# A finished attention tile is scaled on GpSimd instead of VectorE, with double-buffered sums and a signal of its own for the banks

## The chip, the cores and the metric

The kernel runs on one core of a Trainium2 chip. The time is device microseconds (us) of one execution; a kernel's time is the median of its runs. A core has TensorE (PE, matmuls and transposes through its matrix array, into banks of PSUM), VectorE (DVE), ScalarE (ACT), GpSimd (POOL) and SyncE (SP, which here only issues DMAs). Each engine runs its own instructions in order; they order one another by semaphores.

## The reference, cut to what matters

A small language tower: a token embedding; four encoder layers with 12-head attention over a band of 64 keys on either side and a gelu feed-forward; a channel attention; a mixture of four experts; then one layer of full attention with 12 heads of 16 over 256 keys; then a mixture of eight experts. The batch is 8 sequences of 256 tokens, width 192, all float32. The change touches the last step of both attentions:

```
probs = jax.nn.softmax(scores, axis=-1)
out = einsum('bhcqk,bhckd->bhcqd', probs, vb)
```

The kernel doesn't divide the probabilities: it multiplies the exponentials with the values, gets each head's row sum beside them (the values carry a column of ones), and scales the 16 outputs of each head by the reciprocal of the sum afterwards.

## The kernel before, in words

The 2048 tokens are 16 tiles of 128 queries (`NT`); a sequence is two tiles. Attention goes over pairs of heads: 6 pairs to a tile, 96 pairs to a layer, `p` = 0 to 95, in four pair groups of 24 (a group is two sequences, four tiles). It runs five times: banded in the layers called 0 to 3 here, and once dense, with 256 keys. The same code writes the order for every engine:

- TensorE (`pe_attention`), in iteration `p`: scores of pair p (L534, L537), values of pair p-5 (L566 to L568), transposes of the probabilities of pair p-3 (L548), then in some iterations a step (`pe_step`) of work for the next pair group: three "chunks" of queries and keys (k = p mod 24 = 0, 2, 8), four tile transposes (k = 4, 6, 10, 12), four value projections (k = 14, 16, 18, 20). In the last pair group there are none of these; the banded layers have transposes of finished tiles and output projections there instead (`LATE`).
- ScalarE (`act_attention`): the exponentials (L660), and the high parts of the transposed probabilities, `pth` (L670).
- VectorE (`dve_attention`), in iteration p: the row maxima of pair p (`dve_max`, L766), the remainders `ptl` of pair p-4 (`dve_lo`, L772), its share of TensorE's last step, in pairs 6 to 13 of a banded layer the last normalisation of the layer before (`dve_last_norm`, L822 to L831), and then `dve_finish`. That one takes tile t in three parts: at p = 11 + 6t the sums to `rs2` (L786 or L790) and the values to `au` (L791), at p = 12 + 6t the reciprocals (L794), at p = 13 + 6t the scaling to `xn` (L799, 192 columns; L800 repeats the last 64 of them). L800 signals `att_ready`.
- GpSimd: it splits the next group's chunks into three bf16 pieces (`pool_pieces`, L1018 to L1021), which SyncE sends to DRAM and reads back as `qx` and `kx`; it splits the values (`pool_v`, L1084 to L1087), adds residual rows to `hb` (L967), and splits weights for the next stage (`pool_weights`, L999 to L1003: those of `wb` in pair group 1, those of `wa` at the start of pair group 3). Each of them waits, in order, for what it reads.

`att_ready` is waited for by TensorE ahead of the first values of a tile (the bank was used two tiles before), by ScalarE ahead of a tile's first exponential (the maxima of three tiles before), and by TensorE ahead of the transpose of the scaled tile, which comes in the last pair group or after the pairs.

Of the kernel before, what the change touches and what calls it, by code (L numbers as in the profile page):

```python
# [24 lines left out]
ALU = mybir.AluOpType  # L25
# [93 lines left out]
def build_tower(nc, a, out, stop=None):  # L119
    ctx = ExitStack()  # L120
    with ctx:
# [30 lines left out]
        rs2 = sb("rs2", [P, 2, HEADS])  # L152
        au = sb("au", [P, HEADS, DH])
# [14 lines left out]
        tok = au[:, 0, :].bitcast(I32)  # L168
        tokf = qf[:, 0, 0:2 * NT].rearrange("p (a n) -> p a n", a=2)
        toku = au[:, 1, :].bitcast(U32)  # L170
# [117 lines left out]
        att_ready = sig("att_ready", per=NT)  # L288
# [263 lines left out]
        def pe_values(pe, it, p):  # L552
# [4 lines left out]
            if p % 6 == 0:  # L557
                pe.wait_ge(att_ready.sem, att_ready.at(it, 2 * b + qt - 1))
# [90 lines left out]
        def act_exp(act, it, u, banded):  # L649
# [6 lines left out]
            if hd == 0:  # L656
                act.wait_ge(att_ready.sem, att_ready.at(it, tile_no - 2))
# [119 lines left out]
        def dve_finish(dve, ch, it, t, step, banded):  # L777

            r3, r = t % 3, rs2[:, 1, :]
# [56 lines left out]
        def dve_attention(dve, ch, it, banded, tile):  # L836

            for p in range(PAIRS + 8):
# [7 lines left out]
                if p >= 11 and (p - 11) % 6 < 3 and (p - 11) // 6 < NT:  # L846
                    dve_finish(dve, ch, it, (p - 11) // 6, (p - 11) % 6, banded)
# [122 lines left out]
        def pool_tail(pool, ch, it, opening):  # L970
# [9 lines left out]
            scale(1, 0)  # L980
# [24 lines left out]

        def pool_pieces(pool, ch, it, g):

            for i in range(3):
# [13 lines left out]
                pool.wait_ge(next_pieces.sem, next_pieces.at(it, n - 2))  # L1022

# [49 lines left out]
        def pool_v(pool, ch, it, g):  # L1073

            for i in range(4):
# [12 lines left out]
                pool.wait_ge(v3_ready.sem, v3_ready.at(it, n + 1))  # L1088

# [577 lines left out]
        def _(pool):  # L1667
            ch = Chain(ctx, nc, pool, "pool_order", alone)
            for s in (v3_ready, xc_pow_ready, seg_q_ready):
# [25 lines left out]
            def pool_layer(it, opening):  # L1695
# [9 lines left out]
                pool_v(pool, ch, it, 3)  # L1705
# [452 lines left out]
```

## Time and profile before

| | |
|---|---|
| time, median of 3 runs | 1967.51 us (1963.2 to 1977.52) |
| the profiled execution | 1966.12 us, of which the span of the trace is 1964.3 us |
| granted TensorE clock, mean | 0.898 |
| busy over the span | PE 1532.7 us, DVE 1340.6, ACT 1026.9, POOL 712.5 |
| the five stretches of pairs, first to last maximum | 80.4 to 238.5, 351.5 to 508.2, 621.2 to 777.7, 887.3 to 1040.9, 1480.4 to 1628.9 us |

The time of an execution is the trace's span and 1.8 us around it. Busy shares are means over stages with different limits; the rows below are read by stretch. In a timeline row the columns are start, duration, engine, line, operation, what it writes and reads, and in brackets the idle time of the engine just before it with what ended it. Durations of successive instructions of an engine overlap a little, so what an instruction costs is read from start to start.

### The profile page before, as it was taken

The page shows a single profiled execution, that of the slowest core. Times are in us where ns is not written, and L with a number is a line of the kernel's source. Part 1 is how long each engine was busy: PE and PEld are TensorE (multiplying, and loading weights), DVE is VectorE, ACT ScalarE, POOL GpSimd, SP SyncE. Part 2 cuts the span into 40 slices and gives each one's busy share as a digit, 9 for nine tenths or more (in the row PEclk, how much of TensorE's full clock was granted, in tenths as well). Part 3 has the DMA queues.
Part 4 walks back from the last instruction along what each step waited for, and adds up shares of the span by engine and source line. Part 5 has one row for each costly group of instructions (what it writes and reads, how often), then busy time and mean ns, then how long its engine had stood idle before and what let it go on. Part 6 is the DMA issues. An engine that isn't in the chain of part 4 may idle for free.

```text
span 1964.3 us, 45857 instructions
## 1 busy us (share of the span) xinstructions
PE 1532.7 (78%) x14634; PEld 1290.7 (66%) x14634; DVE 1340.6 (68%) x3638; ACT 1026.9 (52%) x2392; POOL 712.5 (36%) x993
## 2 busy tenths in 40 slices
PE   0689889789798898898897938849818886669992
PEld 0467668677677776786776827729816664569992
DVE  4698966789876989668997662253358998344444
ACT  0478733688534787337884313225417883235661
POOL 5554123553134641236531320024525421045541
PEclk9899989899898999899998968769958997679996
DMA  5645101634004451016430000046526430067775
GB/s 130 185 108 115 28 1 31 163 76 87 1 2 128 85 116 28 1 32 160 88 74 1 1 13 1 1 142 189 168 72 140 85 63 23 22 200 241 239 219 173
DMA packets 144329, 178.46 MB, mean 91 GB/s; under 512 B 22096, under 2 KB 106128, under 8 KB 143952
## 3 DMA queue, kind: packets, MB, share of 16 engines
q1 hardware_dynamic: 136784, 158.18, 31.6%
q0 software_dynamic: 7296, 17.18, 2.6%
q8 instruction: 129, 2.11, 0.5%
q14 instruction: 120, 0.98, 0.2%
HBM read 132.96 MB, written 42.34 MB: 89 GB/s over the span
## 4 chain that ended last, share of the span: by engine, by line
PE 31%; DVE 14%; issue 4%; ACT 2%; DMA 2%; POOL 1%; SPq 0%; DVEq 0%; ACTq 0%; POOLq 0%
PE bank L1414 7%; DVE ptl L772 4%; DVE neg_max L766 2%; PE bank L1400 2%; PE bank L548 2%; PE bank L618 2%; DVE xn L886 1%; PE bank L1403 1%; DMA xn<-y_rows 1%; PE bank L1401 1%; PE bank L1402 1%; PE bank L1404 1%; PE bank L423 1%; PE bank L1158 1%; ACT pth L670 1%
## 5 line engine op out<-in xcount | busy, mean ns | idle before, releaser
L660 ACT ACTIVATE prob<-bank,neg_max 128x192 f32<-128x192 f32 (+1 forms) x960 | 408.1, 436 | 132.2 <-DVE neg_max L766 79.0
L772 DVE TENSOR_TENSOR ptl<-bank,pth 128x512 f16<-128x512 f32 x480 | 327.0, 681 | 11.8 <-ACT pth L670 5.6
L766 DVE TENSOR_REDUCE neg_max<-bank 128x2 f32<-128x384 f32 (+1 forms) x480 | 273.4, 570 | 77.5 <-PE bank L537 68.7
L548 PE MATMUL bank<-ident,prob 128*128 128x128 f32 x1920 | 309.6, 285 | 0.0
L670 ACT ACTIVATE pth<-bank 128x512 f16<-128x512 f32 x480 | 284.8, 593 | 7.8 <-PE bank L548 7.5
L566 PE MATMUL bank<-v,pth 128*128 128x33 bf16 x1920 | 200.8, 181 | 106.7 <-DVE ptl L772 89.6
L566 PEld LDWEIGHTS bank<-v,pth 128*128 128x128 f16 x1920 | 154.7, 96 | 190.5 <-DVE ptl L772 177.5
L625 ACT ACTIVATE xx<-bank 128x256 fp32r<-128x256 f32 x256 | 95.7, 387 | 239.8 <-PE bank L423 235.6
L548 PEld LDWEIGHTS bank<-ident,prob 128*128 128x128 f32 x1920 | 205.1, 142 | 0.1
L568 PE MATMUL bank<-v,ptl 128*128 128x33 bf16 x1920 | 194.9, 177 | 0.0
L567 PE MATMUL bank<-v,pth 128*128 128x16 bf16 x1920 | 191.0, 170 | 1.9 <-issue 1.9
L960 POOL TENSOR_SCALAR rstd<-mv 128x4 f32<-128x4 f32 x52 | 12.9, 248 | 446.3 <-DVE mv L876 440.3
L537 PE MATMUL bank<-kx,qx 96*128 96x192 bf16 (+1 forms) x960 | 168.0, 257 | 1.1 <-DVE xx L739 1.1
L567 PEld LDWEIGHTS bank<-v,pth 128*128 128x128 f16 x1920 | 157.6, 97 | 0.1
L568 PEld LDWEIGHTS bank<-v,ptl 128*128 128x128 f16 x1920 | 155.4, 96 | 2.1 <-issue 2.1
L706 ACT ACTIVATE fbuf<-bank,b 128x512 f32<-128x512 f32 x96 | 65.9, 687 | 146.5 <-PE bank L445 146.5
L618 PE MATMUL bank<-w,fbuf 128*128 128x192 f32 x768 | 140.8, 327 | 2.0 <-DVE h L863 2.0
L423 PE MATMUL bank<-ident,xn 128*128 128x128 f32 x256 | 57.3, 339 | 104.6 <-DVE xn L886 54.0
L534 PE MATMUL bank<-mask,ident 128*128 128x384 bf16 x384 | 130.2, 339 | 8.6 <-issue 7.4
L618 PEld LDWEIGHTS bank<-w,fbuf 128*128 128x128 f32 x768 | 128.7, 190 | 12.4 <-issue 5.2
L1337 POOL DMA_INDIRECT y_rows<-vf,mask x68 | 79.6, 1171 | 115.3 <-DVE vf L1491 102.3
L537 PEld LDWEIGHTS bank<-kx,qx 96*128 96x128 bf16 x960 | 95.1, 101 | 35.6 <-issue 4.7
(281 smaller groups left out, 4078.7 us busy)
## 6 DMA issues: line engine op xcount, KB each, us to landing
xn<-in_e_seg SPq DMA_DIRECT2D x34, 768.0 KB, 6.7
w<-in_e_w SPq DMA_DIRECT2D x23, 576.0 KB, 4.2
qk_rows<-fbuf SPq DMA_DIRECT2D x128, 96.0 KB, 2.3
qx<-qk_rows SPq DMA_DIRECT2D x35, 288.0 KB, 4.1
kx<-qk_rows SPq DMA_DIRECT2D x35, 288.0 KB, 5.7
qk_rows<-w SPq DMA_DIRECT2D x80, 96.0 KB, 2.3
qx<-qk_rows SPq DMA_DIRECT2D x35, 192.0 KB, 4.7
kx<-qk_rows SPq DMA_DIRECT2D x35, 192.0 KB, 5.5
```

Source lines behind the costliest of these rows:

```text
L534: nc.tensor.matmul(o, ident_bf, mask[:, 2 * b + qt, :].unsqueeze(1).to_broadcast([P, 2, D]), start=True, stop=False)
L537: last = nc.tensor.matmul(o[:, e, :], qx[0:ROWS, b % 3, hd + e, qt * P:qt * P + P], kx[0:ROWS, b % 3, hd + e, ks], start=not banded, stop= ...
L548: last = nc.tensor.transpose(bank[BT[p % 2]][:, (2 * e + c) * P:(2 * e + c) * P + P], prob[:, qt, hd % PROBS, c * P:c * P + P], ident[:, :])
L566: nc.tensor.matmul(o2, pth[:, p % 3, w], v[:, 0:OC], start=(c == 0), stop=False)
L567: nc.tensor.matmul(o1, pth[:, p % 3, w], v[:, OC:VC], start=False, stop=False)
L568: last = nc.tensor.matmul(o2, ptl[:, p % 2, w], v[:, 0:OC], start=False, stop=(c == 1))
L618: last = nc.tensor.matmul(bank[BY[t]][:, 0:D], fbuf[:, (n - 2) % 4, t * P:t * P + P], w2[:, c, :], start=(c == 0), stop=(c == FC - 1))
L660: nc.scalar.activation(prob[:, qt, hd % PROBS, c0:c0 + n], scores_at(u // 2, n)[:, u % 2, :], ACT.Exp, bias=neg_max[:, tile_no % 3, hd:hd ...
L670: nc.scalar.activation(pth[:, p % 3, :], bank[BT[p % 2]][:, :], ACT.Copy).then_inc(hi_ready.sem, 1)
L766: nc.vector.tensor_reduce(neg_max[:, t % 3, hd:hd + 2], scores_at(p, D if banded else S), AX.X, ALU.max, negate=True).then_inc(max_ready.s ...
L772: nc.vector.tensor_tensor(ptl[:, p % 2, :], bank[BT[p % 2]][:, :], pth[:, p % 3, :], ALU.subtract)\
L1414: last = nc.tensor.matmul(bank[BY[2 * (G % 2) + s]][:, 0:D], fbuf[:, n % 4, s * P:s * P + P], w2_e[G % 3][:, c, :], start=(c == 0), stop=( ...
```

## The change

The two scaling instructions move from `dve_finish` to a new `pool_scale` on GpSimd. `au` and the reciprocals get two buffers, by `t % 2`. VectorE's reciprocal, now the last part of `dve_finish`, signals `sums_ready`; TensorE (bank) and ScalarE (maxima) wait for that instead of `att_ready`. `att_ready` now comes from GpSimd; ahead of a tile's sums VectorE waits until the scaling of two tiles before is done. GpSimd's calls stand at written-out places: tile 0 after the third pieces of pair group 0, tile 1 after its second value split, tiles 2, 3, 4 before the first, after the second and after the third pieces of group 1, tile 5 after its second value split, tiles 6 to 9 likewise in group 2, tile 10 before the weights `wa`, tiles 11 to 15 after them; the reciprocal roots of the first normalisation (`pool_rstd` for (1, 0)) stand between tiles 12 and 13.

```diff
-                act.wait_ge(att_ready.sem, att_ready.at(it, tile_no - 2))
+                act.wait_ge(sums_ready.sem, sums_ready.at(it, tile_no - 2))
...
             if step == 0:
                 dve.wait_ge(pv_done.sem, pv_done.at(it, 6 * t + 6))
+                dve.wait_ge(att_ready.sem, att_ready.at(it, t - 1))
...
-                finish_marks[1] = ch.mark(nc.vector.tensor_reduce(au[:, :, :], ps, AX.X, ALU.add))
+                finish_marks[1] = ch.mark(nc.vector.tensor_reduce(au[:, t % 2, :, :], ps, AX.X, ALU.add))
             elif step == 1:
-                ch.done(finish_marks[0])
-                finish_marks[1] = ch.mark(nc.vector.reciprocal(r, rs2[:, 0, :]))
-            else:
                 ch.done(finish_marks[1])
-                r = r.unsqueeze(2).to_broadcast([P, HEADS, DH])
-                o = xn[:, t, :].rearrange("p (h d) -> p h d", d=DH)
-                nc.vector.tensor_tensor(o[:, 0:HEADS, :], au[:, :, :], r, ALU.mult)
-                nc.vector.tensor_tensor(o[:, HEADS:, :], au[:, 8:HEADS, :], r[:, 8:HEADS, :], ALU.mult)\
-                    .then_inc(att_ready.sem, 1)
+                nc.vector.reciprocal(rs2[:, 1 + t % 2, :], rs2[:, 0, :]).then_inc(sums_ready.sem, 1)
...
+        def pool_scale(pool, it, t):
+
+            if t < 0:
+                return
+            pool.wait_ge(sums_ready.sem, sums_ready.at(it, t + 1))
+            x = au[:, t % 2, :, :]
+            r = rs2[:, 1 + t % 2, :].unsqueeze(2).to_broadcast([P, HEADS, DH])
+            o = xn[:, t, :].rearrange("p (h d) -> p h d", d=DH)
+            nc.gpsimd.tensor_tensor(o[:, 0:HEADS, :], x, r, ALU.mult)
+            nc.gpsimd.tensor_tensor(o[:, HEADS:, :], x[:, 8:HEADS, :], r[:, 8:HEADS, :], ALU.mult)\
+                .then_inc(att_ready.sem, 1)
+
         def pool_pieces(pool, ch, it, g):

+            pool_scale(pool, it, GT * (g - 2) + 2)
             for i in range(3):
...
                 pool.wait_ge(next_pieces.sem, next_pieces.at(it, n - 2))
+                if i > 0:
+                    pool_scale(pool, it, GT * (g - 2) + 2 + i)
...
                 pool.wait_ge(v3_ready.sem, v3_ready.at(it, n + 1))
+                if g and i == 1:
+                    pool_scale(pool, it, GT * (g - 1) + 1)
...
                 pool_v(pool, ch, it, 3)
+                pool_scale(pool, it, NT - 6)
                 pool.wait_ge(rows_x.sem, rows_x.at(it + 1, 48))
...
                 pool_weights(ch, wa, QKV).then_inc(wa_ready.sem, 1)
+                for t in range(NT - 5, NT):
+                    if t == NT - 3:
+                        pool_rstd(pool, ch, it, NORMED.index((1, 0)) + 1, 0, 1e-12)
+                    pool_scale(pool, it, t)
                 pool_tail(pool, ch, it, opening)
```

## Rows read from the trace of the kernel before

**Rows 1.** Busy time by stretch: three pair groups of layer 1, last of dense.

```profile
core 0: us, PE busy (x) PEld busy (x) DVE busy (x) ACT busy (x) POOL busy (x), PEclk, DMA share, GB/s
392.70:432.80 40.10, 35.65 (x497) 29.09 (x495) 36.97 (x81) 32.54 (x84) 24.10 (x32) 1.00 0.43 90
432.80:471.10 38.30, 35.94 (x504) 29.30 (x504) 33.04 (x75) 33.03 (x83) 17.92 (x28) 1.00 0.53 112
471.10:508.20 37.10, 32.21 (x456) 26.83 (x454) 35.25 (x91) 29.59 (x80) 5.58 (x7) 0.95 0.02 4
1596.20:1628.90 32.70, 26.54 (x405) 19.87 (x402) 31.85 (x66) 29.51 (x70) 1.44 (x4) 1.00 0.01 2
```

**Rows 2.** Waits from 351 to 509 us, layer 1's pairs: total, times, longest.

```profile
PEld bank L566 <- DVE ptl L772: 26.9, 52, 2.1
...
DVE neg_max L766 <- PE bank L537: 14.9, 23, 4.1
...
PE bank L566 <- DVE ptl L772: 12.4, 19, 1.9
```

**Rows 3.** VectorE groups by line, whole execution: busy, mean ns, idle before.

```profile
L772 DVE TENSOR_TENSOR ptl<-bank,pth 128x512 f16<-128x512 f32 x480 | 327.0, 681 | 11.8 <-ACT pth L670 5.6
L766 DVE TENSOR_REDUCE neg_max<-bank 128x2 f32<-128x384 f32 (+1 forms) x480 | 273.4, 570 | 77.5 <-PE bank L537 68.7 <-issue 7.1 <-DVEq L113 0.2
...
L799 DVE TENSOR_TENSOR xn<-au,rs 128x192 f32<-128x192 f32 x80 | 33.1, 414 | 0.2
L800 DVE TENSOR_TENSOR xn<-au,rs 128x64 f32<-128x64 f32 x80 | 29.4, 368 | 0.0
```

**Rows 4.** VectorE timeline, layer 1, tile 3's scaling and the wait two maxima on.

```profile
407.85 0.35 DVE L799 TENSOR_TENSOR xn<-au,rs 128x192 f32<-128x192 f32 x1
408.12 0.21 DVE L800 TENSOR_TENSOR xn<-au,rs 128x64 f32<-128x64 f32 x1
408.26 0.55 DVE L766 TENSOR_REDUCE neg_max<-bank 128x2 f32<-128x384 f32 x1
...
410.05 0.56 DVE L766 TENSOR_REDUCE neg_max<-bank 128x2 f32<-128x384 f32 x1 [0.64 <-PE bank L537]
```

**Rows 5.** VectorE timeline, layer 1, tile 2's scaling.

```profile
395.86 1.17 DVE L799 TENSOR_TENSOR xn<-au,rs 128x192 f32<-128x192 f32 x1
396.95 2.25 DVE L800 TENSOR_TENSOR xn<-au,rs 128x64 f32<-128x64 f32 x1
399.12 0.54 DVE L766 TENSOR_REDUCE neg_max<-bank 128x2 f32<-128x384 f32 x1
...
400.19 0.54 DVE L766 TENSOR_REDUCE neg_max<-bank 128x2 f32<-128x384 f32 x1
```

**Rows 6.** GpSimd and ScalarE timelines beside rows 5.

```profile
396.77 2.34 POOL L1003 TENSOR_TENSOR wb_second_lo<-raw,wb_second 64x960 fp32r<-64x960 f32 x1
...
399.70 0.42 ACT L660 ACTIVATE prob<-bank,neg_max 128x192 f32<-128x192 f32 x1 [3.11 <-DVE neg_max L766]
```

**Rows 7.** VectorE timeline, layer 1, tile 6's scaling (next pair group).

```profile
436.40 0.58 DVE L799 TENSOR_TENSOR xn<-au,rs 128x192 f32<-128x192 f32 x1
...
439.05 0.56 DVE L766 TENSOR_REDUCE neg_max<-bank 128x2 f32<-128x384 f32 x1 [0.86 <-PE bank L537]
```

**Rows 8.** VectorE and TensorE timelines, layer 1, tile 10's scaling.

```profile
473.77 0.64 DVE L799 TENSOR_TENSOR xn<-au,rs 128x192 f32<-128x192 f32 x1
...
474.94 0.54 DVE L766 TENSOR_REDUCE neg_max<-bank 128x2 f32<-128x384 f32 x1
```

**Rows 9.** TensorE timeline: waits for VectorE's remainders, three of layer 1, one dense.

```profile
379.19 0.19 PE L566 MATMUL bank<-v,pth 128*128 128x33 bf16 x1 [1.01 <-DVE ptl L772]
...
476.13 0.19 PE L566 MATMUL bank<-v,pth 128*128 128x33 bf16 x1 [1.18 <-DVE ptl L772]
...
494.24 0.19 PE L566 MATMUL bank<-v,pth 128*128 128x33 bf16 x1 [0.23 <-DVE ptl L772]
...
1609.02 0.19 PE L566 MATMUL bank<-v,pth 128*128 128x33 bf16 x1 [0.43 <-DVE ptl L772]
```

**Rows 10.** VectorE timeline at the end of layer 1's pairs.

```profile
518.97 0.36 DVE L799 TENSOR_TENSOR xn<-au,rs 128x192 f32<-128x192 f32 x1
...
519.38 0.35 DVE L863 TENSOR_TENSOR h<-bank,hb 128x192 f32<-128x192 f32 x1
```

**Rows 11.** GpSimd groups by line, whole execution.

```profile
L1085 POOL TENSOR_TENSOR vr<-vf,v 128x192 f32<-128x192 f32 x80 | 44.7, 559 | 14.4 <-POOL v L1084 14.4
...
L1019 POOL TENSOR_TENSOR qf<-qf,fbuf 128x512 f32<-128x512 f32 x30 | 34.9, 1165 | 5.4 <-POOL fbuf L1018 5.4
...
L1708 POOL TENSOR_TENSOR bqk<-bqk,q_scale 128x3 f32<-128x3 f32 x4 | 0.8, 193 | 12.3 <-DMA bqk<-in_bqk 12.3
```

**Rows 12.** GpSimd timeline, third split of a group; its reads on SyncE's queue.

```profile
410.92 0.61 POOL L1018 CAST w<-qf 128x512 bf16<-128x512 f32 x1 [3.39 <-DMA qk_rows<-fbuf]
...
419.64 1.38 SPq L1041 DMA_DIRECT2D kx<-qk_rows  x3
```

**Rows 13.** DMA issues of the page (median us to landing); VectorE timeline at pair 48.

```profile
kx<-qk_rows SPq DMA_DIRECT2D x35, 288.0 KB, 5.7
...
432.82 0.55 DVE L766 TENSOR_REDUCE neg_max<-bank 128x2 f32<-128x384 f32 x1
```

**Rows 14.** VectorE groups by line: the last group's normalisation.

```profile
L822 DVE SCALAR_TENSOR_TENSOR hb<-h,mv,ln_s 128x192 f32<-128x192 f32 x16 | 7.8, 490 | 0.0
L828 DVE SCALAR_TENSOR_TENSOR h<-hb,rstd,ln_b 128x128 f32<-128x128 f32 x16 | 7.6, 473 | 0.0
...
L831 DVE SCALAR_TENSOR_TENSOR h<-hb,rstd,ln_b 128x128 f32<-128x128 f32 x16 | 6.2, 386 | 0.0
```

More of the change, by code:

```diff
@@ L151, in build_tower @@
         neg_max = sb("neg_max", [P, 3, HEADS])
-        rs2 = sb("rs2", [P, 2, HEADS])
-        au = sb("au", [P, HEADS, DH])
+        rs2 = sb("rs2", [P, 3, HEADS])
+        au = sb("au", [P, 2, HEADS, DH])
         stats = sb("stats", [P, NT, 6])
@@ L167, in build_tower @@
         ln_s, ln_b = sb("ln_s", [P, 2, D]), sb("ln_b", [P, 2, D])
-        tok = au[:, 0, :].bitcast(I32)
+        tok = au[:, 0, 0, :].bitcast(I32)
         tokf = qf[:, 0, 0:2 * NT].rearrange("p (a n) -> p a n", a=2)
-        toku = au[:, 1, :].bitcast(U32)
+        toku = au[:, 0, 1, :].bitcast(U32)
         xc_temp = sb("xc_temp", [P, 2])
@@ L287, in build_tower @@
         pv_done = sig("pv_done", per=PAIRS)
-        att_ready = sig("att_ready", per=NT)
+        att_ready, sums_ready = sig("att_ready", per=NT), sig("sums_ready", per=NT)
         o_done = sig("o_done", per=NT)
@@ L557, in pe_values @@
             if p % 6 == 0:
-                pe.wait_ge(att_ready.sem, att_ready.at(it, 2 * b + qt - 1))
+                pe.wait_ge(sums_ready.sem, sums_ready.at(it, 2 * b + qt - 1))
             for e in range(2):
@@ L777, in dve_finish @@
         def dve_finish(dve, ch, it, t, step, banded):
-            r3, r = t % 3, rs2[:, 1, :]
+            r3 = t % 3
             if step == 0:
                 dve.wait_ge(pv_done.sem, pv_done.at(it, 6 * t + 6))
+                dve.wait_ge(att_ready.sem, att_ready.at(it, t - 1))
                 po = bank[BV[t % 2]][:, 0:HEADS * OC].rearrange("p (h c) -> p h c", c=OC)
@@ L845, in dve_attention @@
                     dve_last_norm(dve, ch, it, p)
-                if p >= 11 and (p - 11) % 6 < 3 and (p - 11) // 6 < NT:
+                if p >= 11 and (p - 11) % 6 < 2 and (p - 11) // 6 < NT:
                     dve_finish(dve, ch, it, (p - 11) // 6, (p - 11) % 6, banded)
@@ L978, in sums_of @@
                 pool_hb(pool, it, normed(k, GT * g), g, row_b2[0] if k == 1 else row_bo)
-            scale(1, 0)
             scale(1, 1)
@@ L1668, in _ @@
             ch = Chain(ctx, nc, pool, "pool_order", alone)
-            for s in (v3_ready, xc_pow_ready, seg_q_ready):
+            for s in (att_ready, v3_ready, xc_pow_ready, seg_q_ready):
                 s.start(pool)
@@ L1757, in _ @@
                 pool_v(pool, ch, L, g)
+            pool_scale(pool, L, NT - 6)
             pool.wait_ge(proj_done.sem, proj_done.at(L, ITEMS * NG))
@@ L1760, in _ @@
             pool_weights(ch, wb, D, D).then_inc(seg_q_ready.sem, 1)
+            for t in range(NT - 5, NT):
+                pool_scale(pool, L, t)
             for g in range(NG):
@@ L1833, in _ @@
             ch = Chain(ctx, nc, dve, "dve_order")
-            for s in (xx_ready, vf_ready, max_ready, lo_ready, att_ready, o_read, y_read, xn_ready, xc_norm_ready, xc_k_ready, xc_s_ready, xc_p_ready,
+            for s in (xx_ready, vf_ready, max_ready, lo_ready, sums_ready, o_read, y_read, xn_ready, xc_norm_ready, xc_k_ready, xc_s_ready, xc_p_ready,
                       xc_pt_ready, xc_o_ready, g2_max, sum_ready):
```

## The prediction

> **What bounds the kernel now.** I read first the busy time by stretch. In layer 1 the second pair group lasts 40.1 us with VectorE busy 37.0 and TensorE 35.7; the third lasts 38.3 with TensorE 35.9 and VectorE 33.0; the last lasts 37.1 with VectorE 35.3 and TensorE 32.2; the last group of the dense attention lasts 32.7 with VectorE 31.9 [rows 1]. So there is no one bound: VectorE holds the pairs in groups 1 and 3 and in the dense layer, TensorE in group 2, where its steps for the next group are added. GpSimd is busy 24, 18, 6 and 1 us in the same stretches, the idlest engine by far.
>
> The waits say the same in detail. Over layer 1's pairs TensorE's weight loads wait 26.9 us for VectorE's remainders, and VectorE waits 14.9 us for TensorE's scores [rows 2]. The two alternate: TensorE runs ahead of VectorE in pairs without a step, and VectorE waits for the scores that follow a step. A cut on VectorE pays where TensorE is the next to wait for it, and nothing where VectorE itself waits next. That is the rule by which I place the 80 scalings (16 tiles, five times).
>
> **What leaves VectorE.** L799 and L800, 80 of each, 33.1 + 29.4 = 62.5 us of durations [rows 3]. The durations overlap: an undisturbed pair starts at 407.85 and the next maximum at 408.26, so 0.41 us, not 0.35 + 0.21 = 0.56 [rows 4]. The overlap of 0.15 taken off 80 times leaves 50.5 us that VectorE gives up, 32.8 of it the bare cost and 17.7 stretching. The stretching has places. At tile 2 the pair takes from 395.86 to 399.12, 3.26 us [rows 5], while GpSimd converts the weights `wb`; L800 ends at 399.20, just after GpSimd's 2.34 us subtraction from SBUF ended at 399.11 [rows 6]. At tile 10, beside the weights `wa`, it takes 1.17 us [rows 8].
>
> The Trainium skill (SBUF — State Buffer, Who interferes with whom) states that a VectorE instruction with two SBUF inputs contends with a GpSimd instruction that reads SBUF, and that the later one waits for the whole instruction. The trace agrees at tile 2.
>
> Tile 2. From the scaling's start to the second maximum after it: 400.19 - 395.86 = 4.33 us [rows 5]. Tile 6 stands at the same place of the next group, almost unstretched, and there that maximum waits 0.86 us for TensorE at 439.05, 2.65 us after the scaling's start of 436.40 [rows 7]. So of the 3.26 us given up at least 1.7 is gained before TensorE's chunk ends the wait; the longest waits of TensorE for VectorE in this layer are 1.9 and 2.1 us [rows 2], and ScalarE waits 3.11 us there [rows 6]. I take 2.0. Four banded layers: 8.0 us. The dense layer has no such weights.
>
> Tile 10. TensorE's wait for the remainders beside it is 1.18 us [rows 9], as long as the cost of 1.17 [rows 8], and no wait for TensorE follows closely. Read in the same way, layers 0, 2 and 3 have 0.9, 1.3 and 0.6 us. Sum 4.0.
>
> The other banded scalings cost 0.4 us each, and I gave each the smaller of that and TensorE's next waits. Tile 0: TensorE waits 1.01 us after it in layer 1 [rows 9], likewise in layer 0; the cost is 0.8 there, and 0.1 is to be had in layers 2 and 3: 1.8. Tiles 12 and 13: the wait after tile 12 is 0.23 [rows 9] and a smaller one follows: 0.3 each, 2.4 in four layers. Tiles 1, 5 and 9: some 0.15 each, 1.8. Tile 4: 0.1, so 0.4. Tile 15: its scaling stands at 518.97 straight ahead of the output's residual at 519.38, on which the tail of the layer hangs [rows 10]: 0.4, in four layers 1.6. Tiles 3, 6, 7, 8, 11 and 14: nothing, since the next thing is VectorE's wait for the scores after a step, as the 0.64 us after tile 3's [rows 4]; there the cut becomes idle time. Sum 8.0.
>
> Dense: TensorE waits 0.43 us after a scaling in the last group [rows 9], so tiles 10 to 13 and 15 give 0.4 each, tiles 1, 5 and 9 the same, tiles 0 and 4 0.3, the others nothing: 3.8.
>
> Together 8.0 + 4.0 + 8.0 + 3.8 = 23.8 us.
>
> **What comes to GpSimd.** A scaling is a tensor_tensor on 192 and one on 64 columns. The trace has GpSimd's on 3, 192 and 512 columns at 193, 559 and 1165 ns [rows 11]: about 1.9 ns a column, so 559 and, for 64, some 315: 0.87 us a tile, 70 us in all. None of these rows has an operand repeated by a stride of zero; the bounds are 0.75 us (no stretching) and 2.3 us (two of the 512-column rows), and I take 0.87 by the 192-column row, which is the very shape of the result. It lies beside the pairs, where GpSimd is at most 60% busy [rows 1].
>
> The Trainium skill (GPSIMD Engine Reference, Engine selection) puts a two-input elementwise operation on GpSimd at about twice VectorE's time. The 559 ns against VectorE's 350 of the same 192 columns is a ratio of 1.6; by the page's ratio the pair would take 1.1 us instead of 0.87, and the sum wouldn't move.
>
> What is queued behind the new waits? On GpSimd the calls wait for reciprocals that VectorE makes at pair 12 + 6t. Each is placed near that time. The tightest is group 1, where the scalings of tiles 1, 2 and 3 go ahead of the third pieces. That split started at 410.92 after 3.4 us of idle; its reads were issued from 418 to 421 (the kx reads at 419.64 for 1.4) [rows 12], landing 5.7 us after issue, at 426.7, against their first use at pair 48, 432.8 [rows 13]. So there is room for 3.4 + 6.1 = 9.5 us, and the three scalings need 2.6. On VectorE the new wait at 11 + 6t is for a scaling whose input was ready at 6t, eleven pairs or some 15 us before; queued behind it are the sums, then the next maximum. I cost it at nothing: if the cover were gone, each of the 80 would cost the whole lateness. TensorE's and ScalarE's waits for the banks move to a signal one pair earlier than before, and neither waits there now. One semaphore wait more at the sums replaces one at the scaling: zero, between -0.05 and +0.05 us a tile, 4 us either way.
>
> **The sum.** The profiled execution took 1966.1 us (span 1964.3 and 1.8 around it), 1.4 under the median of the runs. 1966.1 - 23.8 = 1942.3; on the median's scale 1943.7.
>
> **Rivals.**
>
> A, TensorE takes over. Where I count 0.1 to 0.4 us a tile, TensorE's next step may eat everything, as it does at tile 3. Then only the stretching at tiles 2 and 10 comes back, 8.0 + 4.0 = 12 us: 1955.5. For it: group 2 is TensorE's already [rows 1]. Against: TensorE waits 26.9 us in a layer for VectorE [rows 2].
>
> B, everything pays. If VectorE's lead is carried over TensorE's steps, 45 to 50 us come back: 1920. For it: the last groups with VectorE 95 to 97% busy [rows 1]. Against: the 0.64 and 0.86 us for which VectorE waits now just after a scaling [rows 4, 7].
>
> C, the shared port only changes hands. GpSimd reads SBUF 70 us more beside the pairs. VectorE's remaining instructions there with two SBUF inputs are the last group's normalisation in pairs 6 to 13, means of 490, 473 and 386 ns, the last two on the same number of elements and so some of it stretching already [rows 14], and the four-tile normalisation at pair 98. Tile 0's scaling moves the rows for `hb` behind it, onto pair 13. At most two scalings a layer can be waited for in full, and three of the `hb` rows: 2 x 0.87 + 3 x 0.6 = 3.5 us, four times 14. That gives 23.8 - 14 = 10: 1957.5. The Trainium skill (Perfetto Trace Analysis, Optimizing Scalar/DVE Operations) warns that moving work between these two engines might not help because they share an SBUF read port; by that rule the time would be this rival's.
>
> D, slower: the scalings hold up GpSimd's queue. If a scaling on GpSimd costs x instead of 0.87, the pieces of group 1 come late by 3x - 9.5, so TensorE's scores of pair 48 wait for `kx` from x = 3.2 on, five times; the next group, with more idle ahead of its pieces, follows later. At x = 6 that is 8.5 x 5 = 42 us lost against 24 gained: 1985. It needs an operation that costs five times what its neighbours in the trace cost.
>
> **How the numbers follow.** This kernel's own runs spread by 0.7%, so about 1% is what can be told from no change. Forecast, 1930 to 1952: 0.60. A 0.15, B 0.10, C 0.10, D 0.05. Faster by over 1% means below 1947.8: B whole and most of the forecast, 0.10 + 0.52 = 0.62, and a small part of A, 0.64. Slower by over 1% is D, 0.05. The rest, 0.31, is within 1%. The range takes in A, C and the near side of B: 1924 to 1961.
>
> **What the next profile should show.** L799 and L800 gone from VectorE; the maximum after tile 2's reciprocal no longer late, and group 1 as long as group 2, about 38 us; group 3 about 35.5. GpSimd's new lines at 0.56 and 0.32 us, ending well before VectorE's sums two tiles on, with no VectorE wait on them. VectorE's waits for scores up by some 20 us in total, TensorE's for the remainders down by as much. I would be wrong on the size if the waits for scores rise by nearly 50 (A), wrong on the cover if VectorE's sums wait for GpSimd or the scores for `kx` (D), and wrong on the port if L822 to L831 or L906 grow (C).

## The result, and the profile after

The changed kernel takes 1954.67 us (median of 11 runs, 1951.03 to 1961.94), the kernel before, on the same chip, 1970.52 us (11 runs). The ratio of the runs is 0.9932, with a 95% interval of 0.9915 to 0.995: 13.4 us less, between 10 and 17 (the two medians by themselves are 15.9 apart, inside this interval). Run again later on another chip (the last table of the experiments), it gave 0.9917 [0.989, 0.9943]. So the sign was forecast rightly, and the gain of 23.8 us was nearly twice too large.

From the page of the changed kernel, the busy times and two groups that answer to [rows 3, 11]:

```profile
span 1957.5 us, 45898 instructions
## 1 busy us (share of the span) xinstructions
PE 1539.4 (79%) x14634; PEld 1296.5 (66%) x14634; DVE 1297.1 (66%) x3478; ACT 1033.0 (53%) x2392; POOL 772.0 (39%) x1153
...
L766 DVE TENSOR_REDUCE neg_max<-bank 128x2 f32<-128x384 f32 (+1 forms) x480 | 274.3, 572 | 102.8 <-PE bank L537 97.3
...
L1007 POOL TENSOR_TENSOR xn<-au,rs 128x192 f32<-128x192 f32 x80 | 41.0, 512 | 197.7 <-DVE rs L795 195.6
```

VectorE is busy 43.5 us less, GpSimd 59.5 us more. The scaling costs GpSimd 512 ns for 192 columns, and L1008's 64 columns cost 294. GpSimd stands idle ahead of it for VectorE's reciprocals; for the scaling itself one transpose of TensorE waits 0.3 us in the whole execution, and nothing else does. But VectorE's waits for TensorE's scores (L766 for L537) are up from 68.7 to 97.3 us [rows 3].

Layer 1's second, third and last pair groups and the last of the dense attention, as in [rows 1] (busy time of each engine, then granted clock, DMA share, GB/s):

```profile
390.10:428.30 38.20, 35.50 (x494) 29.06 (x493) 32.41 (x73) 32.84 (x85) 26.74 (x40) 1.00 0.47 95
428.30:467.10 38.80, 35.85 (x504) 29.38 (x504) 31.45 (x68) 33.19 (x83) 20.87 (x36) 1.00 0.53 108
467.10:501.60 34.50, 31.13 (x456) 25.45 (x453) 32.88 (x84) 29.62 (x79) 8.53 (x15) 1.00 0.03 7
1586.20:1617.80 31.60, 26.54 (x405) 19.85 (x402) 31.03 (x58) 29.56 (x69) 4.76 (x12) 1.00 0.01 3
```

The second group went from 40.1 to 38.2 us and is TensorE's now (35.5 busy against VectorE's 32.4). The third did not get shorter, though VectorE gave up 1.6 us of work in it. The last went from 37.1 to 34.5, of which 1.0 is a fall of TensorE's clock that in this layer only the profile of before has (mean granted clock 0.95 there [rows 1]); the dense one went from 32.7 to 31.6. The waits over layer 1's pairs, as in [rows 2]:

```profile
PEld bank L566 <- DVE ptl L772: 23.7, 55, 1.5
DVE neg_max L766 <- PE bank L537: 23.6, 28, 3.5
...
PE bank L566 <- DVE ptl L772: 7.9, 14, 1.3
```

TensorE's weight loads wait 3.2 us less for the remainders and its matmuls 4.5 us less. A weight load and the matmul behind it wait through mostly the same idle time; counted once, it is 4.1 us. VectorE waits 8.7 us more for scores. At tile 2, where the scaling took 3.26 us [rows 5], VectorE now has:

```profile
393.19 0.56 DVE L766 TENSOR_REDUCE neg_max<-bank 128x2 f32<-128x384 f32 x1
...
395.81 0.56 DVE L766 TENSOR_REDUCE neg_max<-bank 128x2 f32<-128x384 f32 x1 [1.46 <-PE bank L537]
...
405.52 0.56 DVE L766 TENSOR_REDUCE neg_max<-bank 128x2 f32<-128x384 f32 x1 [1.03 <-PE bank L537]
```

The maxima run on, and the wait in the first bracket is for TensorE's chunk of queries and keys. That wait is what takes the place of the stretching. The last row answers to the 0.64 us of [rows 4], at tile 3: the wait for scores there has grown to 1.03.

To place the gain I took the starts of the 480 maxima (L766) and added up the time from one to the next over stretches of six pairs. Each stretch of six holds one scaling of before. Changed minus before, in us:

| pairs of a layer (tile scaled there before) | layers 0 to 3 | sum | forecast | dense |
|---|---|---|---|---|
| 12 to 17 (0) | +0.40, +0.29, -0.01, +0.03 (clock: see below) | +0.7 | -1.8 | -0.15 |
| 24 to 29 (2) | -3.11, -1.81, -1.81, -1.76 | -8.5 | -8.0 | -0.04 |
| 72 to 77 (10) | -0.79, -1.03, -1.18, -0.51 | -3.5 | -4.0 | -0.25 |
| 84 to 89 (12) | -0.20, -0.19, -0.20, -0.20 | -0.8 | -1.2 | -0.25 |
| 90 to 94 (13) | -0.08, -1.40, -0.39, -0.39 | -2.3 | -1.2 | -0.32 |
| 18 to 23, 30 to 47, 54 to 71, 78 to 83 (1, 3 to 5, 7 to 9, 11) | within 0.04 each | 0 | -2.2 | -0.9 |

Left out are pairs 0 to 11 and 48 to 53, whose length varies from layer to layer in both kernels. The dense column adds to -1.9 where -3.8 was forecast.

Two rows hold falls of the granted clock. In pairs 90 to 94 it fell in layers 0 and 1 of before and in layer 0 of the changed kernel; without that each layer has -0.39, the sum is -1.6. In pairs 12 to 17 it fell for some 3 us in layers 2 and 3 of before and in all four layers of the changed kernel. Where it fell in both, the difference is -0.01 and +0.03. Where it fell in neither, which the run of the complement below shows for the same order of work, the stretch takes 10.33 or 10.34 us against 10.43 before. So tile 0 gave nothing with the fall and 0.1 us a layer without it, and the +0.7 is the clock; whether the change itself makes the fall more frequent there no run shows. The table's mechanisms together are 8.5 + 3.5 + 0.8 + 1.6 + 1.9 = 16.3 us, inside the interval of the measurement. All stretches of pairs, from the start of the first maximum to that of the last, took 773.2 us before and 757.1 after.

The two spans differ by less, 1964.3 and 1957.5 us, because single executions differ between the pairs. Between the banded layers and the dense attention, where both kernels issue the same instructions, the one profile of before has 439.6 us and the eleven of the changed kernel and the variants 438.9 to 449.7; after the last maximum 335.4 and 336.4 to 346.7. The profile of before happens to lie at the low end of both. So stretches of pairs are compared below, with the timed ratios beside them.

### The profile page after: what moved, and what is told of

Same layout as the page of the kernel before. It is cut to its first block, busy times and chain, and to the rows that moved or that the text cites. A ratio compares the mean times of both kernels' runs of the same rounds, so it can differ in the third digit from the quotient of the medians.

```text
span 1957.5 us, 45898 instructions
## 1 busy us (share of the span) xinstructions
PE 1539.4 (79%) x14634; PEld 1296.5 (66%) x14634; DVE 1297.1 (66%) x3478; ACT 1033.0 (53%) x2392; POOL 772.0 (39%) x1153
## 4 chain that ended last, share of the span: by engine, by line
PE 32%; DVE 13%; issue 4%; ACT 2%; DMA 2%; POOL 1%; SPq 0%; DVEq 0%; ACTq 0%; POOLq 0%
PE bank L1424 7%; DVE ptl L772 3%; PE bank L548 2%; PE bank L1410 2%; DVE xn L880 1%; PE bank L618 1%; DVE neg_max L766 1%; PE bank L1413 1%; PE bank L1412 1%; PE bank L1411 1%; PE bank L1414 1%; PE bank L423 1%; PE bank L1168 1%; PE bank L566 1%; DMA xn<-y_rows 1%
## 5 line engine op out<-in xcount | busy, mean ns | idle before, releaser
L766 DVE TENSOR_REDUCE neg_max<-bank 128x2 f32<-128x384 f32 (+1 forms) x480 | 274.3, 572 | 102.8 <-PE bank L537 97.3
L537 PE MATMUL bank<-kx,qx 96*128 96x192 bf16 (+1 forms) x960 | 167.9, 256 | 1.2 <-DVE xx L739 1.1
L1007 POOL TENSOR_TENSOR xn<-au,rs 128x192 f32<-128x192 f32 x80 | 41.0, 512 | 197.7 <-DVE rs L795 195.6
```

What stands on the lines that cost most here:

```text
L537: last = nc.tensor.matmul(o[:, e, :], qx[0:ROWS, b % 3, hd + e, qt * P:qt * P + P], kx[0:ROWS, b % 3, hd + e, ks], start=not banded, stop= ...
L766: nc.vector.tensor_reduce(neg_max[:, t % 3, hd:hd + 2], scores_at(p, D if banded else S), AX.X, ALU.max, negate=True).then_inc(max_ready.s ...
```

## The experiments

Two questions. Is the gain the stretched scalings of tiles 2 and 10, or the 0.41 us of each? And is it the move to another engine that brings it, or only that VectorE's instruction no longer meets GpSimd's long ones?

**Only tiles 2 and 10 move.** The changed kernel, with `dve_finish` keeping the scaling of the other 14 banded tiles and of the dense ones:

```diff
+        def on_pool(t, banded):
+            return banded and t in (2, 10)
...
+            elif not on_pool(t, banded):
+                dve.wait_ge(sums_ready.sem, sums_ready.at(it, t + 1))
+                dve.wait_ge(att_ready.sem, att_ready.at(it, t))
...
+                nc.vector.tensor_tensor(o[:, 0:HEADS, :], x, r, ALU.mult)
```

> The changed kernel, but only tiles 2 and 10 of the banded layers are scaled on GpSimd; the other 14 tiles of those layers and all 16 dense ones are scaled on VectorE again, from the double buffers. Group lengths are from first maximum to the next group's first maximum in layer 1 (before 41.2, 40.1, 38.3, and 37.1 from pair 72 to 95; changed kernel 41.5, 38.3, 38.8, 34.5). Theory T (the gain is the stretching at tiles 2 and 10, where VectorE waits for GpSimd's conversion of weights; elsewhere VectorE's waits for the scores eat what it gives up): groups 1 and 2 at 38.3 and 38.3 to 38.8, the last at 35 to 35.5, time 11 to 12 us under the kernel before. Rival P (each scaling moved pays its 0.4 us or a good part): groups 1 and 2 come out 1 to 1.6 us longer than in the changed kernel, time no more than 6 to 8 us under before.

Measured: 1961.24 against 1974.1 us, ratio 0.9928 [0.9898, 0.9957]. The second groups last 38.2 us in all four banded layers, as in the changed kernel; the stretches of pairs add to 762.6 us. Tile 3's scaling, back on VectorE, is the first shown here (VectorE's timeline):

```profile
401.55 0.53 DVE L805 TENSOR_TENSOR xn<-au,rs 128x192 f32<-128x192 f32 x1
...
402.14 0.54 DVE L766 TENSOR_REDUCE neg_max<-bank 128x2 f32<-128x384 f32 x1
...
403.73 0.56 DVE L766 TENSOR_REDUCE neg_max<-bank 128x2 f32<-128x384 f32 x1 [0.45 <-PE bank L537]
```

It costs 0.59 us from start to start, and a wait for scores of 0.45 still follows two maxima on. Without it, in the changed kernel, that wait is 1.03 us: the cut and the wait change places one for one. Eight scalings of 80 carry, within the interval, the whole measured gain; by the stretches they give the same 8.5 + 3.5 us as in the changed kernel. This run also has the double buffers and the new signals at every tile, and its stretches with the other tiles are those of before to 0.04 us wherever the clock held: buffers and signals bring nothing by themselves.

**The complement.** The same edit turned round, `return not banded or t not in (2, 10)`: 72 scalings on GpSimd, tiles 2 and 10 of the banded layers on VectorE.

> The complement: the changed kernel with tiles 2 and 10 of the banded layers scaled on VectorE again, all others on GpSimd. Theory T: group 1 of layer 1 stays at 40 us, as before, the pair group from pair 72 keeps about 1 us of its 2.6, L799's counterpart at tile 2 is stretched to 3 us for the two, and the time is 2 to 5 us under before. Rival P: 8 us or more under before.

Measured: 1967.85 against 1974.1 us, 0.9965 [0.9948, 0.9982], pairs 765.4 us. Tile 2 in layer 1:

```profile
393.73 1.19 DVE L805 TENSOR_TENSOR xn<-au,rs 128x192 f32<-128x192 f32 x1
394.84 2.25 DVE L806 TENSOR_TENSOR xn<-au,rs 128x64 f32<-128x64 f32 x1
397.02 0.55 DVE L766 TENSOR_REDUCE neg_max<-bank 128x2 f32<-128x384 f32 x1
```

The stretching is there as in [rows 5], 3.29 us, and the second groups last 40.1 us as before. What 72 scalings bring is 0.35% with an interval of 0.2 to 0.5%, half of what eight bring. (The two parts add to 1.07%, more than the 0.68% of the whole; the three intervals are wide enough for both. By the stretches, 12.0 us and the 0.8 + 1.6 + 1.9 that this profile repeats make the 16.3 of the whole.)

**The weights wait instead.** The kernel before, with nothing moved: GpSimd waits until tile 2's scaling (tile 10's) is done before it converts the second (the first) weight.

```diff
                 pool.wait_ge(rows_y.sem, rows_y.at(it, 16 * 8))
+                pool.wait_ge(att_ready.sem, att_ready.at(it, 3))
                 alone(pool)
...
                 pool.wait_ge(rows_x.sem, rows_x.at(it + 1, 48))
+                pool.wait_ge(att_ready.sem, att_ready.at(it, 11))
                 alone(pool)
```

> The kernel before, all scaling on VectorE, with two waits added on GpSimd: it starts the weights wb only when tile 2 is scaled, and the weights wa only when tile 10 is. Theory T (contention of the two engines for a port): no scaling on VectorE takes longer than 0.7 us for its two instructions at those places; group 1 of layer 1 at 38.3, the last at 36; time 9 to 12 us under before, that is most of the change's gain without moving any work. Rival: it is VectorE's work itself that counts and the long durations are an artefact of the record: time as before, within 3 us. If the pieces behind the weights come late, the scores of pair 48 wait and group 2 starts late, by up to 3 us a layer.

Measured: 1960.82 against 1974.1 us, 0.9933 [0.9906, 0.996], pairs 759.1 us. VectorE's timeline at tile 2:

```profile
390.42 0.35 DVE L799 TENSOR_TENSOR xn<-au,rs 128x192 f32<-128x192 f32 x1
390.69 0.22 DVE L800 TENSOR_TENSOR xn<-au,rs 128x64 f32<-128x64 f32 x1
...
393.07 0.56 DVE L766 TENSOR_REDUCE neg_max<-bank 128x2 f32<-128x384 f32 x1 [1.10 <-PE bank L537]
```

and GpSimd's beside it:

```profile
391.07 0.99 POOL L999 CAST wb_hi<-raw 128x960 fp32r<-128x960 f32 x1 [4.25 <-DVE xn L800]
...
393.17 2.22 POOL L1002 TENSOR_TENSOR wb_lo<-raw,wb_hi 128x960 fp32r<-128x960 f32 x1 [0.18 <-POOL wb_second L1000]
```

The scaling takes 0.40 us instead of 3.26. GpSimd stood idle 4.25 us for it, and nothing was late for that. Two waits on GpSimd give, within the intervals, the same ratio as the whole change. That GpSimd's instructions cause the stretching is now more than an argument from two rows that lie side by side: the same instructions on the same engine lose it when GpSimd's come later. And they hand it on, since GpSimd's weights now lie beside tile 3's scaling:

```profile
400.61 1.20 DVE L799 TENSOR_TENSOR xn<-au,rs 128x192 f32<-128x192 f32 x1
...
401.86 0.54 DVE L766 TENSOR_REDUCE neg_max<-bank 128x2 f32<-128x384 f32 x1
```

That is 1.25 us instead of 0.41. Of the 14.1 us less in the pairs, the six-pair stretches give tile 2 8.5 and tile 10 2.4, and take back 1.1 at tile 3, 0.26 to 0.35 a layer; the rest of the 0.84 us there comes out of VectorE's waits, which are shorter by 0.5. What is left of the 14.1 isn't ascribed to the edit: the first six pairs are 2.0 us shorter (in layer 1 and the dense layer their clock is below full for a shorter time), a clock fall less in the last groups is 1.2, a gap of TensorE at pair 48 that this profile lacks is 2.2 (last section), and pairs 6 to 17 are 1.1 longer. So by the same sums the changed kernel is some 6 us better than this one, which the two ratios, each known to 0.2 or 0.3%, can't show.

**Shorter weight instructions.** The kernel before, with the weights converted in two halves of their columns (960 as twice 480):

```diff
+            if c1 > D:
+                for a0, a1 in ((0, c1 // 2), (c1 // 2, c1)):
+                    last = pool_weights_part(ch, w, a1 - a0, c0 + a0, a0)
+                return last
+            return pool_weights_part(ch, w, c1, c0, 0)
```

> The kernel before, all scaling on VectorE, with GpSimd's conversion of the weights wa and wb done in two halves of the columns, so that no GpSimd instruction there is longer than 1.2 us instead of 2.3. If VectorE's instruction waits until the GpSimd instruction that holds the port has ended, the stretching at tile 2 is bounded by what is left of one short instruction each: L799 and L800 together 1.2 to 2.3 us there instead of 3.4, group 1 of layer 1 at 38.5 to 39.3 instead of 40.1, time 4 to 8 us under before. If instead the two engines share the port in proportion to what they read, the total stays at 3.4 and the time as before.

Measured: 1959.76 against 1967.07 us, 0.996 [0.9946, 0.9973], pairs 763.8 us. Tile 2 on VectorE:

```profile
391.97 0.54 DVE L799 TENSOR_TENSOR xn<-au,rs 128x192 f32<-128x192 f32 x1
392.43 0.60 DVE L800 TENSOR_TENSOR xn<-au,rs 128x64 f32<-128x64 f32 x1
```

The next maximum starts at 392.95. GpSimd has:

```profile
391.09 1.20 POOL L1012 TENSOR_TENSOR wb_second_lo<-raw,wb_second 64x480 fp32r<-64x480 f32 x1
392.24 0.70 POOL L1008 CAST wb_hi<-raw 128x480 fp32r<-128x480 f32 x1
```

The scaling takes 0.98 us instead of 3.26 (0.89 to 0.98 in the four layers), though GpSimd's work is the same in sum, and L800 ends at 393.03, just after the cast at 392.94. What VectorE loses goes by the single GpSimd instruction that it meets, not by GpSimd's sum. How much of the difference is the length, and how much that the second one met is a cast of 0.70 us and not a subtraction, isn't separated. The second groups are at 38.3 us, all of tile 2's part recovered; tile 10's pairs, 72 to 77, give 1.5 us in four layers, against 2.4 with the waits.

**The rows for `hb` first.** In the changed kernel tile 0's scaling moved behind the `hb` rows of the last group:

```diff
                 pool_hb(pool, it, normed(2, NT - GT) - 2 * NT, NG - 1, row_bo)
+                pool_scale(pool, it, 0)
                 pool_v(pool, ch, it, 1)
```

> The changed kernel with tile 0 of the banded layers scaled after the four hb rows instead of before them. In the changed kernel the hb rows run beside the normalisation on VectorE at pair 13, whose two instructions take 0.71 and 0.68 us there; this placing should give back 0.33 us each. Theory T with the port (rival C of the prediction at this one place): pair 13 takes 2.0 to 2.1 us instead of 2.69, group 0 of layer 1 is 0.3 to 0.7 us shorter, time 1 to 2 us under the changed kernel, which the medians can't resolve. Otherwise pair 13 stays at 2.7.

Measured: 1962.15 against 1974.1 us, 0.9926 [0.9896, 0.9956]. In the changed kernel GpSimd's row addition falls onto the normalisation's last two instructions, on VectorE

```profile
373.67 0.71 DVE L822 SCALAR_TENSOR_TENSOR h<-hb,rstd,ln_b 128x128 f32<-128x128 f32 x1
374.30 0.68 DVE L825 SCALAR_TENSOR_TENSOR h<-hb,rstd,ln_b 128x128 f32<-128x128 f32 x1
```

beside GpSimd's

```profile
373.08 1.74 POOL L961 TENSOR_TENSOR hb<-h,row_bo 128x192 f32<-128x192 f32 x3
```

and with the order turned round VectorE has

```profile
372.55 0.34 DVE L822 SCALAR_TENSOR_TENSOR h<-hb,rstd,ln_b 128x128 f32<-128x128 f32 x1
372.81 0.34 DVE L825 SCALAR_TENSOR_TENSOR h<-hb,rstd,ln_b 128x128 f32<-128x128 f32 x1
```

Pair 13 takes 1.98 us instead of 2.69 in all four layers. It carries through pairs 12 to 17 in layers 1 and 3 (9.62 us), but layers 0 and 2 have 10.64 and 10.72, as in the changed kernel. The granted clock tells the two kinds apart. Layers 1 and 2 from pair 13 on:

```profile
371.10:374.60 3.50, 3.10 (x50) 2.50 (x45) 3.50 (x10) 2.68 (x9) 1.32 (x3) 1.00 0.87 169
637.80:641.30 3.50, 3.50 (x33) 3.25 (x30) 3.14 (x9) 2.74 (x8) 1.31 (x3) 0.51 0.88 171
```

In layer 2 TensorE is at half clock for these 3.5 us and busy all through; VectorE's 0.7 us bring nothing there. At full clock the same pairs take 10.43 us before, 10.34 with tile 0 moved (the complement's run) and 9.62 here. So the move with the `hb` rows in their old place is worth 0.8 us a layer at full clock, and the rows on pair 13 take 0.7 of it back. Both are too small for the timed ratio.

**GpSimd leaves the scaling out.** The changed kernel with both instructions of `pool_scale` replaced by the signal alone, so the output of both attentions isn't scaled (what is written to `xn` is missing):

```diff
-            nc.gpsimd.tensor_tensor(o[:, 0:HEADS, :], x, r, ALU.mult)
-            nc.gpsimd.tensor_tensor(o[:, HEADS:, :], x[:, 8:HEADS, :], r[:, 8:HEADS, :], ALU.mult)\
-                .then_inc(att_ready.sem, 1)
+            pool.sem_inc(att_ready.sem, 1)
```

> The changed kernel with GpSimd's two scaling instructions left out (their signal is kept); the attention's output is not scaled or written, so the time shows what the scaling costs where it now stands. Theory T (on GpSimd it is covered, except at tile 0 where it pushes the hb rows onto VectorE's normalisation): groups 1, 2 and the last within 0.1 us of the changed kernel's 38.2, 38.8 and 34.5 in layer 1, pair 13 at 2.0 to 2.4 us instead of 2.69, time within 3 us of the changed kernel. Rival C (GpSimd's reads of SBUF or its lateness hold up VectorE in many places): groups 1 to 3 shorter by 0.5 us or more each, time 8 us or more under the changed kernel.

Measured: 1954.63 against 1967.07 us, 0.9938 [0.9918, 0.9959], pairs 752.8 us. Taking 64.5 us of work off GpSimd gives nothing that the timing can tell (the changed kernel had 0.9932). The six-pair stretches agree with the changed kernel within 0.05 us apart from the first group, pair 48 and the clock's falls. Pairs 12 to 17 are shorter by 0.84, 0.74, 0.74 and 0.88 us, but not by the work alone: in the changed kernel the clock falls there in all four layers, here in none. Against the full-clock stretches of the complement (10.34 us) the 9.98 here are 0.36 less, and pair 13 takes 2.34 us instead of 2.69. So the work costs some 0.35 us a layer on its new engine, 1.4 us in all, at tile 0, where the last normalisation stands.

**The normalisation spread out.** If VectorE now has idle time in the pairs, work that is crowded can go there. In the changed kernel the eight pieces of the last group's normalisation move from pairs 6 to 13 to pairs 7, 8, 13 to 16, 19 and 20, and GpSimd's `hb` rows go behind its first value splits:

```diff
-            if not 6 <= p < 6 + 2 * GT:
+            places = (7, 8, 13, 14, 15, 16, 19, 20)
+            if p not in places:
                 return
-            t = NT - GT + (p - 6) // 2
-            if p == 6:
+            n = places.index(p)
+            t = NT - GT + n // 2
+            if n == 0:
...
-                pool_hb(pool, it, normed(2, NT - GT) - 2 * NT, NG - 1, row_bo)
                 pool_v(pool, ch, it, 1)
+                pool_hb(pool, it, normed(2, NT - GT) - 2 * NT, NG - 1, row_bo)
```

> The changed kernel with the last group's normalisation on VectorE spread from pairs 6 to 13 over pairs 7, 8, 13, 14, 15, 16, 19 and 20, where VectorE waits for TensorE's steps in the groups that have no normalisation, and GpSimd's four hb rows after the value splits instead of before them. If what counts is VectorE's lateness at pairs where TensorE waits for it, group 0 of layers 1 to 3 gets 1 to 2.5 us shorter (41.5 to 39.5 or so in layer 1), likewise layer 0, time 4 to 9 us under the changed kernel. If TensorE's steps fill those pairs already, the length stays within 0.5 us.

Measured: 1947.38 (1945.85 to 1949.69) against 1967.07 us, 0.9894 [0.9876, 0.9913], pairs 746.3 us. The normalisation's pieces are short, as this one (VectorE's timeline, layer 1):

```profile
360.74 0.34 DVE L824 SCALAR_TENSOR_TENSOR h<-hb,rstd,ln_b 128x128 f32<-128x128 f32 x1
```

The first groups of the five layers add to 193.2 us against 202.0 in the changed kernel. Most of it, 7.4 us, is in pairs 6 to 11, from which the normalisation left. In pairs 12 to 17 the clock held in all four layers; of the 3.7 us less there some 2.0 remain against the complement's full-clock 10.34, and the rest is the falls that this profile lacks.

**Is the move needed for that?** The spread normalisation and the two waits for the weights, both in the kernel before, with every scaling left on VectorE. It ran on one chip with the changed kernel and with the version above once more.

> The kernel before with two edits and no scaling moved: GpSimd waits for tile 2's (tile 10's) scaling before it converts the second (first) weight, and the last group's norm of the projection is spread over pairs 7, 8, 13 to 16, 19 and 20, with GpSimd's bias rows issued after its first splits. Theory T (the move to GpSimd itself is worth only the dense layer's 2.4 us and some 1 us in the last groups): groups 1 at 38.5, last groups at 35.3, group 0 near 38 to 40, the ratio 0.990 to 0.993, 2 to 5 us above the version with the spread norm and scaling on GpSimd when both run on one chip. Rival (the move is what makes room in group 0 for the spread norm): group 0 gives nothing, the ratio is 0.993 or worse.

> The changed kernel once more, beside the others on one chip. Every theory: ratio 0.992 to 0.994. It sets what the two other kernels of this call are compared with.

> The changed kernel with the last norm spread over the pairs, once more on the same chip as the version that leaves all scaling on VectorE. Theory T: ratio 0.989 to 0.990, so 5 to 8 us below the changed kernel and 2 to 5 us below the version on VectorE. Rival (its first time was the chip's, not the kernel's): ratio 0.992 to 0.994, level with the changed kernel.

Measured, against 1980.3 us for the kernel before:

| | us | ratio | pairs, us | first groups | last groups |
|---|---|---|---|---|---|
| spread, scaling on VectorE | 1963.59 | 0.993 [0.9901, 0.9959] | 758.0 | 197.6 | 177.0 |
| changed kernel again | 1960.94 | 0.9917 [0.989, 0.9943] | 758.2 | 202.4 | 172.4 |
| spread, scaling on GpSimd | 1946.58 | 0.9842 [0.9808, 0.9875] | 747.4 | 193.6 | 172.2 |

My theory T, that the move itself is worth 2 to 5 us, fell: the medians are 17 us apart (the two intervals leave some 9 either way), 10.6 of them in the pairs. The rival was right on the ratio. On group 0 it was only half right: without the move the spread does not give nothing there, the first groups are 197.6 us against 201.8 before, and 193.6 with the move. The spread takes up VectorE's idle time in pairs 12 to 22 of the first group, and then every scaling there pays. VectorE's timeline in layer 1 of the version with the scaling on VectorE, tile 1:

```profile
376.87 0.41 DVE L824 SCALAR_TENSOR_TENSOR hb<-h,mv,ln_s 128x192 f32<-128x192 f32 x1
377.20 0.50 DVE L799 TENSOR_TENSOR xn<-au,rs 128x192 f32<-128x192 f32 x1
...
377.76 0.55 DVE L766 TENSOR_REDUCE neg_max<-bank 128x2 f32<-128x384 f32 x1
```

From pair 12 to pair 22 no row of it has a bracket: VectorE never waits, and tile 1's scaling costs 0.56 us. In six-pair stretches of layers 0 to 3 the version on VectorE is slower than the one on GpSimd by 0.55, 0.40, 0.40 and 0.40 us in pairs 12 to 17 (tile 0), by 0.85, 0.84, 0.85 and 0.63 in 18 to 23 (tile 1), by 0.27 at tile 3 (1.26 us long beside the weights that wait), 0.28 at tile 10, 0.2 at tile 12 and 0.39 at tile 13 (where the clock held), and by 1.9 in the dense layer. With 4.9 us from tiles 0 and 1, 4 x 1.14 from the four others and 1.9 that is 11.4 us. The last version against the changed kernel on the same chip is 1946.58 / 1960.94 = 0.993, 14.4 us, 10.8 of them in the pairs. It is the fastest version here. What is not in the pairs lies in stretches where both issue the same instructions, and isn't ascribed.

## Why the prediction was right in sign and wrong in size

**Tiles 2 and 10, right.** Forecast 8.0 and 4.0 us, measured 8.5 and 3.5. The stretching was read rightly, the price too: at tile 2 not the 3.26 us of the pair but what is left before TensorE's chunk ends the next wait. The runs with two tiles moved and with waiting weights show that it is this mechanism, and the split weights that it goes by GpSimd's single instruction. Within the term the sharing differs: layer 0 gave 3.11 and the others 1.8.

**Tiles 12 and 13, right.** Forecast 2.4, measured 2.4 where the clock held (0.8 and 1.6, forecast as 1.2 and 1.2).

**Tiles 0, 1, 4, 5, 9 and 15, wrong; this is the step that failed.** "The other banded scalings cost 0.4 us each, and I gave each the smaller of that and TensorE's next waits." Forecast 1.8 + 1.8 + 0.4 + 1.6 = 5.6 us, measured nothing. There are three reasons. The rule itself failed at tiles 1, 4, 5 and 9 (2.2 us of the forecast). It took a wait of TensorE for a remainder as proof that VectorE sets the pace there. But when a maximum ends earlier TensorE still has to get through its own next step, and the cut comes out again as a wait for the scores further on: the six-pair stretches of these tiles have the same length to 0.02 us, and VectorE's waits for L537 in them rose from 0.2, 0.4, 0.2 and 0.4 us to 0.6, 1.0, 0.6 and 0.8 (layers 0 to 2). The right question is what ends the whole stretch up to the next step of TensorE, and there VectorE already waited for L537 in the profile of before, in layers 0 to 2; in layer 3 it waited at tile 4 alone, and nothing was gained at the others either. Tile 3 was judged so, and rightly; the same test was owed to the others.

Tile 15 failed for another reason. The tail looked as if it hung on the scaling, which stood straight ahead of the residual with no idle time between [rows 10]. In the changed kernel:

```profile
512.19 0.23 DVE L795 RECIPROCAL rs<-rs 128x12 f32<-128x12 f32 x1
...
512.64 0.36 DVE L857 TENSOR_TENSOR h<-bank,hb 128x192 f32<-128x192 f32 x1 [0.22 <-PE bank L455]
```

The residual now waits for TensorE's projection, and the time from the last maximum of layer 1 to the first of layer 2 is 113.0 us before and 113.1 after. Two things without idle time between them are in order, but the later one need not depend on the earlier.

**Tile 0, the gain taken back.** Forecast 1.8, measured nothing. Here the rule named a gain that exists: with the `hb` rows ahead of the scaling the pairs 12 to 17 are 0.8 us a layer shorter than before where the clock holds. Rival C named what eats it: the scaling pushes the `hb` rows onto pair 13, which takes 0.7 us back, a cost that the sum put at nothing. Where the clock falls at pair 13, neither shows (10.7 us in either kernel), and which layers those are changes from profile to profile. Of C's other part, scalings that GpSimd's reading of SBUF holds up elsewhere, nothing shows. The Trainium skill (Perfetto Trace Analysis, Optimizing Scalar/DVE Operations) doubts that moving work between these two engines helps, because they share an SBUF read port. The rows agree where GpSimd's work meets VectorE's normalisation, at pair 13 (0.71 and 0.68 us instead of 0.34), and not for the other 76 scalings.

**Dense, half.** Forecast 3.8, measured 1.9: in the last group each scaling within the pairs gave 0.25 to 0.32 us, not 0.4, and those of tiles 0, 1, 4, 5 and 9 0.15, not 0.3 or 0.4. Why the dense layer keeps a part where the banded ones keep none was not tried.

**GpSimd's side, right.** 0.51 + 0.29 = 0.81 us against 0.87 forecast. No wait of VectorE for the scaling and none for `kx` shows, so D did not happen; the run without the scaling bounds its whole cost. The waits for scores rose by 28.6 us. The prediction's signs for that were loose: of 50.5 us given up, 23.8 come back in its sum and 12 in A's, which leaves 26.7 and 38.5 us to become waits, not "some 20" and "nearly 50". TensorE's waits for the remainders fell by 13.6 us at the weight loads and 18.4 at the matmuls; as the two lie mostly in the same idle time, counted once they fell by 17 to 18.

So the sum was 8.0 + 4.0 + 2.4 that held, and 9.4 of small terms (5.6 banded, 3.8 dense) that came out as 1.9. The time fell next to rival A's 1955.5, and A's reason, that TensorE takes over, holds for the banded tiles except 0, 12 and 13. A's gain of 12 us lies within the measured 10 to 17, the forecast's 23.8 does not. The 0.15 that I gave it was too little.

## What to carry to other kernels

Where an instruction takes several times its usual length, look at what a neighbouring engine runs beside it. Before moving it to another engine, move the neighbour, or cut it into shorter ones: here two waits on the idlest engine brought, by the timed ratios, what the move of 80 operations brought. For each cut ask who ends the stretch up to the next fixed step, not whether someone waits for the engine once nearby; many small terms that rest on one untested rule are one term, and want one range. Before a difference of a few tenths of a us between two profiles is read as the change's, compare the granted clock of the two stretches. Work taken off an engine where another sets the pace brought nothing by itself here, and paid once the room was used: the same move gave 2 us beside the waiting weights (759.1 against 757.1 in the pairs; 6 by the stretches that one can ascribe) and 11 with the normalisation spread out.

## What the runs showed of the hardware that was not expected

**A half clock within busy stretches.** In some last groups, of other layers in each execution (in one of none), pairs 91 and 92 take 2.1 and 1.9 us instead of 1.5 and 1.2 and the stretch of pairs 90 to 94 about 7.9 instead of 6.5 (1.4 us; with the scaling on VectorE 1.0). Windows over the end of layer 0 in the changed kernel, with the granted clock behind the busy times:

```profile
218.00:223.00 5.00, 4.81 (x77) 3.86 (x76) 4.78 (x12) 4.55 (x12) 0.76 (x2) 1.00 0.02 5
223.00:228.00 5.00, 3.81 (x56) 3.08 (x52) 5.00 (x18) 3.51 (x10) 1.27 (x2) 1.00 0.01 3
228.00:232.00 4.00, 3.38 (x39) 2.96 (x37) 3.43 (x9) 3.14 (x8) 0.76 (x2) 0.61 0.02 4
```

A mean of 0.61 over 4 us is some 3 us at 1.2 GHz and the rest at 2.4. In the 5 us before it TensorE was busy 3.81 us where it had been 4.81. Layers 1 to 3 went through the same order of work at full clock in this execution. The same happens at pair 13, for some 3 us at 1.2 GHz (once twice as long): in 22 of the 36 banded layers of the nine profiles with the normalisation in pairs 6 to 13, and in none of the 12 with it spread out. What TensorE did before doesn't tell the layers apart: in the 5.2 us before pair 13 of layer 1 it was busy 3.33 us in the changed kernel, where the clock then fell, and 3.34 us in the complement's run, where it held. Why one layer and not another is open.

**A gap of TensorE that nothing explains.** At the first values of pair group 2, in some layers and executions:

```profile
429.00 0.17 PE L567 MATMUL bank<-v,pth 128*128 128x16 bf16 x1 [0.82 <-issue]
```

It lengthens pair 48 by up to 1.1 us. The profile of before has it in three layers (2.3 us in all), the changed kernel in three (3.0), the runs with waiting weights and with the scaling on VectorE in none, and the fastest version in two layers of one profile (0.6) and in none of the other. Its cause was not tried.
